# Gathers of four features for 32 batch rows each, released chunk by chunk, with the first half's layers 2 and 3 moved among the last chunks of a DLRM tower

## The reference

```
e = stack([tbl_f[ids[:, f]] for f in 0..25], axis=1)        # 512 x 26 x 128
combined = concatenate([dense[:, None, :], e], axis=1)       # 512 x 27 x 128
inter = einsum('bfd,bgd->bfg', combined, combined)
z = concatenate([dense, inter[:, iu, ju]], axis=1)           # pairs i < j
h = concatenate([z, dense], axis=1)                          # 512 x 607
h = maximum(h @ W_top1 + b_top1, 0)                          # 512
h = maximum(h @ W_top2 + b_top2, 0)                          # 256
y = h @ W_top3                                               # 1
```

## Time and profile before

| | |
|---|---|
| time, median of 3 runs | 138.34 us (137.31 to 138.55) |
| the profiled execution's span | 161.6 us |
| PE busy in it | 113.8 us (70%), 674 matmuls |
| PEld busy | 98.9 us (61%) |
| DVE busy | 85.1 us (53%) |
| POOL busy | 71.7 us (44%), 64 gathers among it |
| ACT busy | 65.7 us (41%) |
| mean granted TensorE clock | 0.873 of full speed |

### The profile page before, as it was taken

The page is one execution under the profiler, slowest core; times in us unless marked ns, Lnnn a source line. Parts: engine busy times, 40 slices in busy tenths (PEclk is TensorE's granted clock), DMA queues, the critical chain, the costliest instruction groups (busy, mean ns, idle before and its releaser), DMA issues.

```text
span 161.6 us, 1858 instructions
## 1 busy us (share of the span) xinstructions
PE 113.8 (70%) x674; PEld 98.9 (61%) x674; DVE 85.1 (53%) x162; ACT 65.7 (41%) x109; POOL 71.7 (44%) x72
## 2 busy tenths in 40 slices
PE   5499996995980997580000798762999697944994
PEld 5378774884860885570000897761999666943992
DVE  5399989997896370010000648966055731365031
ACT  3286994894894050200000657362133341332112
POOL 2687787878778777777770055710000000000000
PEclk9999999999998589967555569999699999996599
DMA  4998974797396221122110001110000000000000
GB/s 108 234 370 322 253 252 119 214 232 209 88 398 227 62 56 49 49 54 60 49 49 16 0 16 49 41 28 0 0 0 4 0 0 0 4 0 0 0 0 1
DMA packets 6331, 14.59 MB, mean 90 GB/s; under 512 B 1842, under 2 KB 2354, under 8 KB 6195
## 3 DMA queue, kind: packets, MB, share of 16 engines
q1 hardware_dynamic: 4130, 10.23, 20.4%
q0 software_dynamic: 2048, 4.20, 9.7%
q10 hardware_dynamic: 144, 0.05, 0.2%
HBM read 14.47 MB, written 0.00 MB: 90 GB/s over the span
## 4 chain that ended last, share of the span: by engine, by line
PE 34%; POOL 21%; issue 13%; another core or an unknown queue 11%; DVE 9%; DMA 6%; ACT 4%; DVEq 0%; ACTq 0%
POOL e_rows L345 21%; PE gram L413 15%; PE late L453 8%; DMA e_rows<-in_tbl,idx 3%; DMA idx<-in_ids_rows 2%; PE look L395 2%; DVE flip L748 2%; DVE flat L750 2%; ACT pT_hi L561 2%; PE late L385 2%; PE look L474 1%; PE late L386 1%; DVE dots L543 1%; ACT dots L561 1%
## 5 line engine op out<-in xcount | busy, mean ns | idle before, releaser
L345 POOL DMA_INDIRECT e_rows<-in_tbl,idx x64 | 70.8, 1107 | 33.0 <-issue 18.6
L413 PE MATMUL gram<-eT 128*123 128x108 f32 x256 | 32.9, 294 | 23.0 <-DVE dots L543 19.3
L413 PEld LDWEIGHTS gram<-eT 128*123 128x123 f32 x256 | 32.1, 210 | 23.8 <-ACT dots L561 17.9
L385 PE MATMUL late<-onehot,table_hi 128*128 128x512 f32 x84 | 35.3, 420 | 4.0 <-DVE table_lo L684 2.4
L691 DVE TENSOR_SCALAR onehot<-ids,row_of_partition 128x512 fp32r<-128x512 int32 x72 | 30.4, 483 | 7.5 <-PE late L386 5.8
L386 PE MATMUL late<-onehot,table_lo 128*128 128x512 f32 x84 | 34.1, 406 | 0.0
L543 DVE COPY dots<-gram 32x216 f32<-32x216 f32 (+1 forms) x32 | 12.3, 384 | 30.9 <-remote 18.3
L561 ACT ACTIVATE dots<-gram 32x216 f32<-32x216 f32 x32 | 10.9, 340 | 40.2 <-remote 22.2
L385 PEld LDWEIGHTS late<-onehot,table_hi 128*128 128x128 f32 x84 | 16.6, 198 | 8.4 <-ACT table_hi L561 2.7
L386 PEld LDWEIGHTS late<-onehot,table_lo 128*128 128x128 f32 x84 | 16.7, 198 | 3.2
L395 PE MATMUL look<-ident,e_rows 128*128 128x128 f32 x64 | 10.7, 294 | 6.7 <-DMA e_rows<-in_tbl,idx 6.3
(11 more groups left out here) (51 smaller groups left out, 110.2 us busy)
## 6 DMA issues: line engine op xcount, KB each, us to landing
table<-in_tbl SPq DMA_DIRECT2D x7, 512.0 KB
ids<-in_ids_bcast SPq DMA_DIRECT2D x10, 256.0 KB
table<-in_tbl SPq DMA_DIRECT2D x2, 640.0 KB
w_raw<-in_w SPq DMA_DIRECT2D x1, 1280.0 KB
e_rows<-in_tbl,idx POOLq DMA_INDIRECT x64
table<-in_tbl SPq DMA_DIRECT2D x2, 256.0 KB, 5.7
w_raw<-in_w SPq DMA_DIRECT2D x1, 512.0 KB
x_rows<-in_dense SPq DMA_DIRECT2D x1, 256.0 KB
```

The lines of the kernel that those rows point to most:

```text
L345: pool.indirect_dma_start(out=e_rows[:, n % GROUPS_AHEAD, s % GROUP, :], out_offset=None, in_=tables[f][:, :], in_offset=bass.IndirectOffs ...
L385: pe.matmul(bank, table_hi[0:KP, i % 2, c, :], hot, start=c == 0, stop=False)
L413: last = pe.matmul(gram[0:ROWS_OUT, n % 2, q, 0:QUADS * NG_COL], eT_flat[:, b * SLOTS:b * SLOTS + ROWS_OUT], eT[:, b:b + QUADS, 0:NG_COL], ...
```

## The change

Each gather now fetches, for 32 batch rows, four features: 128 rows again, from one table `gathered` in which the 16 tables stand one behind the other. Four gathers make a group, and group c holds all 16 features of chunk c. The host orders the ids that way and gives each feature's first row beside them; DVE adds the two before the first gather. `gram_chunk(n)` replaces `gram_tile(t)` and waits for the groups up to n alone. Groups 0 to 4 are turned behind tables 1 to 5, groups 5 to 7 behind tables 7 to 9, the others among the chunks. Layer 3 uses the `look` banks. The orders of PE, ACT and DVE behind the tables are written anew. DVE's and ACT's loops over tables use `AFTER_TABLE` in the same places where they used `EARLY`, and `w_split(k)` is the weight splitting that stood in `dots_tile`.

```diff
 
-GROUP, GROUPS_AHEAD = 4, 5
-GROUPS = [list(range(a, min(a + GROUP, NG))) for a in range(0, NG, GROUP)]
-NGR = len(GROUPS)
+GROUPS_AHEAD = 5
+UNIT = 32
+NCK = B // UNIT
+PER_GATHER = P // UNIT
+GROUP = NG // PER_GATHER
+assert GROUP * PER_GATHER == NG and NG * UNIT == B
...
-ALL_GROUPS = [(t, g) for t in range(TILES) for g in range(NGR)]
-FIRST_TABLE = 1
-EARLY = ALL_GROUPS[:NOH - FIRST_TABLE]
-REST = {t: [(t, g) for g in range(NGR) if (t, g) not in EARLY] for t in range(TILES)}
-
-AFTER_TABLES = [g for t in range(TILES) for g in REST[t]]
-assert len(AFTER_TABLES) == 7
-BESIDE_GRAM = {0: [None, None, AFTER_TABLES[0], None], 1: [None, AFTER_TABLES[1], None, None],
-               2: [AFTER_TABLES[3], None, None, AFTER_TABLES[4]], 3: []}
-AFTER_DENSE, AFTER_LAYER2, LAST_GROUPS = AFTER_TABLES[2:3], AFTER_TABLES[5:6], AFTER_TABLES[6:]
-
-
-def looks(ks):
-    return [("group", *k) for k in ks if k]
-
-
-LOOK_ORDER = [("dense",)] + looks(EARLY) + looks(BESIDE_GRAM[0]) + looks(BESIDE_GRAM[1])
-LOOK_ORDER += [("turn", 0)] + looks(AFTER_DENSE) + [("turn", 1)] + looks(BESIDE_GRAM[2])
-LOOK_ORDER += [("layer2", 0, n) for n in range(N2)] + looks(AFTER_LAYER2) + [("turn", 2)] + looks(LAST_GROUPS)
-LOOK_ORDER += [("turn", 3)] + [("layer2", 1, n) for n in range(N2)]
+AFTER_TABLE = {1: 0, 2: 1, 3: 2, 4: 3, 5: 4, 7: 5, 8: 6, 9: 7}
+
+
+LOOK_ORDER = [("dense",)] + [("group", c) for c in AFTER_TABLE.values()]
+LOOK_ORDER += [("group", 8), ("group", 9), ("turn", 0), ("group", 10), ("group", 11), ("turn", 1)]
+LOOK_ORDER += [("group", 12), ("turn", 2), ("layer2", 0, 0), ("layer2", 0, 1), ("group", 13), ("layer3", 0)]
+LOOK_ORDER += [("group", 14), ("group", 15), ("turn", 3)]
+LOOK_ORDER += [("layer2", 1, 0), ("layer2", 1, 1), ("layer3", 1)]
 LOOK = {what: n for n, what in enumerate(LOOK_ORDER)}
-assert FIRST_TABLE == 1 and all(("group", *k) in LOOK for k in ALL_GROUPS)
+assert [k[1] for k in LOOK_ORDER if k[0] == "group"] == list(range(NCK))
 
...
 for _h in range(HALVES):
-    LATE_ORDER += [("layer1", _h, 0), ("layer1", _h, 1), ("layer3", _h)]
+    LATE_ORDER += [("layer1", _h, 0), ("layer1", _h, 1)]
 LATE = {what: n for n, what in enumerate(LATE_ORDER)}
...
-            pool.wait_ge(idx_in, 16)
-            for t, g in ALL_GROUPS:
-                n = t * NGR + g
-                if n >= GROUPS_AHEAD:
-                    wait_look_full(pool, ("group", *ALL_GROUPS[n - GROUPS_AHEAD]))
-                for s in GROUPS[g]:
-                    f = GATHERED[s]
+            pool.wait_ge(idx_ready, 1)
+            for c in range(NCK):
+                if c >= GROUPS_AHEAD:
+                    wait_look_full(pool, ("group", c - GROUPS_AHEAD))
+                for k in range(GROUP):
+                    n = c * GROUP + k
                     pool.indirect_dma_start(
-                        out=e_rows[:, n % GROUPS_AHEAD, s % GROUP, :], out_offset=None, in_=tables[f][:, :],
-                        in_offset=bass.IndirectOffsetOnAxis(ap=idx[:, t, f:f + 1], axis=0)
-                    ).then_inc(rows_in[t][g], 16)
+                        out=e_rows[:, c % GROUPS_AHEAD, k, :], out_offset=None, in_=gathered[:, :],
+                        in_offset=bass.IndirectOffsetOnAxis(ap=idx[:, n:n + 1], axis=0)
+                    ).then_inc(rows_in[c], 16)
...
-            def turn_group(t, g):
-                bank = look_bank(("group", t, g))
-                pe.wait_ge(rows_in[t][g], 16 * len(GROUPS[g]))
-                for k, s in enumerate(GROUPS[g]):
-                    last = pe.transpose(bank[:, k * P:(k + 1) * P], e_rows[:, (t * NGR + g) % GROUPS_AHEAD, k, :], ident[:, :])
+            def turn_group(c):
+                bank = look_bank(("group", c))
+                pe.wait_ge(rows_in[c], 16 * GROUP)
+                for k in range(GROUP):
+                    last = pe.transpose(bank[:, k * P:(k + 1) * P], e_rows[:, c % GROUPS_AHEAD, k, :], ident[:, :])
                 last.then_inc(look_full, 1)
 
-            def gram_tile(t):
-
-                upto = LOOK["group", t, NGR - 1]
-                if t == 0:
+            def gram_chunk(n):
+
+                upto = LOOK["group", n]
+                if n == 0:
                     wait_late_done(pe, ("table", NOH - 1))
                     pe.wait_ge(pads_ready, 1)
                 pe.wait_ge(look_act, len([w for w in LOOK_ACT if LOOK[w] <= upto]))
                 pe.wait_ge(look_dve, len([w for w in LOOK_DVE if LOOK[w] <= upto]))
-                for c in range(NCH):
-                    n = t * NCH + c
-                    if n >= 2:
-                        pe.wait_ge(dots_act, n - 1)
-                        pe.wait_ge(dots_dve, n - 1)
-                    for q in range(CHUNK_Q):
-                        b = t * P + (c * CHUNK_Q + q) * QUADS
-                        last = pe.matmul(gram[0:ROWS_OUT, n % 2, q, 0:QUADS * NG_COL],
-                                         eT_flat[:, b * SLOTS:b * SLOTS + ROWS_OUT],
-                                         eT[:, b:b + QUADS, 0:NG_COL], start=True, stop=True)
-                    last.then_inc(gram_full, 1)
-                    if c < len(BESIDE_GRAM[t]) and BESIDE_GRAM[t][c]:
-                        turn_group(*BESIDE_GRAM[t][c])
+                if n >= 2:
+                    pe.wait_ge(dots_act, n - 1)
+                    pe.wait_ge(dots_dve, n - 1)
+                for q in range(CHUNK_Q):
+                    b = n * UNIT + q * QUADS
+                    last = pe.matmul(gram[0:ROWS_OUT, n % 2, q, 0:QUADS * NG_COL],
+                                     eT_flat[:, b * SLOTS:b * SLOTS + ROWS_OUT],
+                                     eT[:, b:b + QUADS, 0:NG_COL], start=True, stop=True)
+                last.then_inc(gram_full, 1)
...
-                bank = late_bank(("layer3", h))
+                bank = look_bank(("layer3", h))
...
+                if i == 0:
                     turn_dense()
-            gram_tile(0)
-            gram_tile(1)
+            gram_chunk(0)
+            gram_chunk(1)
+            turn_group(8)
+            gram_chunk(2)
+            gram_chunk(3)
+            gram_chunk(4)
+            gram_chunk(5)
+            turn_group(9)
+            gram_chunk(6)
             turn_pairs(0)
+            gram_chunk(7)
+            turn_group(10)
+            gram_chunk(8)
+            gram_chunk(9)
+            turn_group(11)
+            gram_chunk(10)
+            turn_pairs(1)
             layer1_dense(0)
-            groups(AFTER_DENSE)
-            turn_pairs(1)
+            gram_chunk(11)
             layer1_pairs(0)
-            gram_tile(2)
+            turn_group(12)
+            gram_chunk(12)
+            turn_pairs(2)
             layer2(0)
-            groups(AFTER_LAYER2)
-            turn_pairs(2)
+            turn_group(13)
+            gram_chunk(13)
             layer3(0)
             layer1_dense(1)
-            groups(LAST_GROUPS)
-            gram_tile(3)
+            turn_group(14)
+            gram_chunk(14)
+            turn_group(15)
+            gram_chunk(15)
             turn_pairs(3)
             layer1_pairs(1)
             layer2(1)
             layer3(1)
...
-            copy(eT[:, t * P:(t + 1) * P, s:s + n],
-                 look[:, LOOK[what] % 2, 0:n * P].rearrange("d (f b) -> d b f", f=n)).then_inc(done, 1)
+            copy(eT[:, c * UNIT:(c + 1) * UNIT, 1:1 + NG],
+                 look[:, LOOK[what] % 2, :].rearrange("d (f b) -> d b f", f=NG)).then_inc(done, 1)
...
                                    ACT.Relu, bias=b2_sb[:, n:n + 1]).then_inc(look_act, 1)
 
-            dots_tile(0)
-            dots_tile(1)
+            for n in range(6):
+                dots_chunk(n)
+                w_split(n)
+            group(9)
+            dots_chunk(6)
+            w_split(6)
             turn_hi(0)
-            groups(AFTER_DENSE)
+            dots_chunk(7)
+            w_split(7)
+            dots_chunk(8)
+            dots_chunk(9)
+            group(11)
+            dots_chunk(10)
             turn_hi(1)
+            dots_chunk(11)
             h1_split(0)
-            dots_tile(2)
+            dots_chunk(12)
+            turn_hi(2)
             h2_relu(0)
-            groups(AFTER_LAYER2)
-            turn_hi(2)
-            groups(LAST_GROUPS)
-            dots_tile(3)
+            group(13)
+            dots_chunk(13)
+            dots_chunk(14)
+            group(15)
+            dots_chunk(15)
             turn_hi(3)
             h1_split(1)
...
+            dve.wait_ge(idx_in, 16)
+            dve.tensor_tensor(idx[:, :], idx_parts[:, 0, :], idx_parts[:, 1, :], ALU.add).then_inc(idx_ready, 1)
...
-                wait_late_full(dve, ("layer3", h))
-                copy(y[0:1, h * HB:(h + 1) * HB], late[0:1, LATE["layer3", h] % 2, 0:HB]).then_inc(late_dve, 1)
-
-            dots_tile(0)
+                wait_look_full(dve, ("layer3", h))
+                copy(y[0:1, h * HB:(h + 1) * HB], look[0:1, LOOK["layer3", h] % 2, 0:HB]).then_inc(look_dve, 1)
+
```

(43 more changed lines are left out.)

103 lines of the change are left out of this document (47 added, 56 removed).

## The result

The changed kernel takes 135.62 us in the median (132.2 to 138.84, 4 runs) beside 138.44 for the kernel before (137.31 to 138.66, 4 runs): a ratio of 0.966, 95% interval 0.954 to 0.977. It is faster, by 2.8 us in the median where 4.9 were forecast, and its runs lie much further apart than those of the kernel before. The profiled execution was the shortest, 132.2 us, with a span of 130.2 us.

What follows compares the result with a forecast made beforehand. PE was taken as bound by gathers up to Gram, then by waits for DVE and ACT. -5.9 for Gram's start and +1.0 for waits make -4.9: 138.34 becomes 133.4, forecast's own range 131.9 to 134.9, whole range 130.2 to 139.0.

Steps and rivals of the forecast that it cites:

- The start of Gram: End of the tables: one group less turned there moves Gram from 64.3 to 58.4, -5.9, between -7.0 and -3.7.
- The last link: Before Gram: group 7's rows land at 57.9, are turned by 58.3, and Gram starts at 58.4.
- The add: DVE's index addition of 64 integers per partition before the gathers: delays all of them by 0.2 us.
- The 4.15: At table 8: transposes of 0.4 and 16 products at 0.23 at full clock, against 6.7 us in the trace.
- The waits: PE behind Gram's start: 9.6 us removed, 10.2 added, 0.4 for one more group; net +1.0, from -1.5 to +3.
- group 8: Turned behind chunk 1: rows land at 63.1, PE is there at 62.0, a wait of 1.1 us.
- rival A: PE's clock falls again behind new waits, 1.7 to 2.3 per spell: 135.4 with one, 137.5 with two; chance 0.2.
- a stretch of 0.7: Gathers 30 and 31 beside table 9's one-hots on DVE take 0.35 longer each, 0.7 together, range 0 to 1.4.
- put together: The kernel before, its profile reckoned without the stop: Gram at 64.3, span 137.1 instead of 161.6.
- C: Rival: the 4.33 us wait before table 8 isn't in the timed runs, so 139.0; chance 0.13.
- D: Rival: gathers from one table of some 187,000 rows lose pace; 0.3 more per gather gives 143; chance 0.10.
- B: Rival: new waits overlap better (-1.5) or gathers land in 2 us (-1): 131; chance 0.15.

Runs made afterwards that it cites:

- before, again: The kernel before, unchanged, run and profiled a second time: 139.0 us, span 137.3.
- shift alone: The kernel before with only group 5 turned behind table 7, 6 behind 8, 7 behind 9, 8 behind chunk 1: 136.64 us median beside 139.13.
- nine groups: The changed kernel with nine groups turned behind tables 1 to 9 as before, all else kept: 140.34 us median, ratio 1.020.
- changed, second: The changed kernel, unchanged, run and profiled again: 135.47 us median (7 runs) beside 139.13, ratio 0.974; profiled span 137.2.
- old order: The changed kernel with the order behind the tables put nearly back to that of the kernel before: 135.38 us, ratio 0.984.
- new order: The changed kernel with layer 2(0) moved ahead of group 12 and the turning of pairs 2: 132.0 us, ratio 0.960.
- group 4 later: The changed kernel with group 4 turned behind table 6 instead of table 5: 137.88 us, ratio 0.978.
- best: The changed kernel with layer 2(0) earlier, group 13's copy ahead of turn_hi(2) on ACT, and identity products in PE's waits: 131.52 us beside 138.01.

## Why the prediction was right, and where its sizes were off

| kernel | 32nd gather's issue ends | Gram starts | Gram to the end | span |
|---|---|---|---|---|
| before, again | 55.00 | 64.89 | 72.4 | 137.3 |
| shift alone | 54.20 | 56.62 | 78.7 | 135.3 |
| nine groups | 52.21 | 61.88 | 74.4 | 136.3 |
| changed, first | 53.57 | 56.55 | 73.65 | 130.2 |
| changed, second | 57.30 | 60.75 | 76.45 | 137.2 |
| old order | 54.79 | 57.22 | 74.3 | 131.5 |
| new order | 54.13 | 57.21 | 72.3 | 129.5 |
| group 4 later | 58.30 | 60.95 | 76.9 | 137.8 |
| best | 54.61 | 57.20 | 69.7 | 126.9 |

**The start of Gram.** -5.9 forecast, -8.3 in the first profile (64.89 to 56.55), -4.1 in the second: the second inside the bounds of 3.7 and 7.0, the first beyond them. The main mechanism is as told: the long wait and the half clock behind it are gone in the first profile. The last link isn't. The forecast let Gram's start hang on the rows of group 7, the 32nd gather. Gram does begin 2.4 to 3.5 us behind that gather's issue in all rows of the table with eight groups, but PE waits for group 7 for 0.37 us at most (the shift alone), and in neither profile of the changed kernel. There the last wait for rows is that for group 6 (0.78, first) or for group 4 (4.39, second); behind it come PE's own tables and ACT's copy of table 9. In the first profile all of this was early: the turning of group 6 began at 51.13 (52.5 reckoned), and table 9's copy ended at 56.50 (57.9). The issue of the 32nd gather ended 1.7 us earlier than reckoned (53.57 for 55.24), although one of the gathers beside the last one-hots took 2.02; the turning then began 1.7 us behind it where I had taken 2.7.

**The add** took 0.23 us (0.2 forecast), and the first gather starts at 4.85 (5.1). The 4.15 that the prediction has for group 6's turning and table 8 at full clock is 4.1 by its own terms (0.4 and 16 x 0.23); nothing hangs on the difference.

**The waits.** 10.02 us for the forecast's 10.2; Gram to the end 73.65 for 73.8. That is partly luck in the parts: chunks 6 and 10 and layer 2 wait longer (1.48, 1.88, 2.49 for 0.8, 1.3, 2.0), group 8 and chunk 13 less (0 and 0.72 for 1.1 each); chunks 12, 14 and 15 are within 0.2 (1.62, 0.83, 1.00 for 1.8, 0.85, 1.2). Group 8 was in time: its rows were there by 60.27, where I had 63.1, and 1.7 us of that is how early the gathers were. That the order costs about what it saves fits the kernels with one half of the change: nine groups with the new gathers, release and order are +1.2 in the median (+1.0 forecast), but the same three are -1.2 when they are added to the shift, and the order isn't to be seen when the old one is put back behind the new gathers. All three are near what six runs can tell.

**The clock, rival A.** The chance was too low, and the price of 1.7 to 2.3 for a spell a little too high. The forecast held against A that none of the new waits reaches 3.4 us alone. In the second profile the clock fell twice behind shorter ones, at chunk 10 and at layer 2(0), the second being a place that A names; such spells cost 1.4 to 1.6 us each in the profiles that have one. At layer 2(0), with the order as in the changed kernel, the wait of 2.45 to 2.49 was followed by one in three profiles of six. The same wait of 1.88 or 1.89 us before chunk 10 (1.90 in one) was followed by a chunk of 1.94 us in five profiles and of 2.22, 2.42, 2.94 and 3.51 us in four others; the wait of 3.48 before pairs 3 is followed by half clock in all twelve profiles in which PE is idle in it (the 36 products take 5.86 to 7.32 us) and in neither of the two in which it is kept busy (4.54 and 4.56). Whether a short wait is punished changes from execution to execution.

**What the forecast lacked.** It treated the gathers' pace as one number with a stretch of 0.7. A gather that is held up for 4.4 us was not in the trace of the kernel before, where the longest of those among the tables takes 2.41, and my range of 0 to 1.4 for the stretching was too small (the two gathers beside the last one-hots took 1.68 and 3.60 in the second profile, 3.4 more than twice 0.94). The second profile of the kernel before has such a gather too (4.39), and there it cost little: the 20th gather's issue ends at 36.87 instead of 35.93, the 32nd's at 55.00 instead of 54.34, and the span is the one put together without it. In the changed kernel's two profiles the 20th ends at 33.78 and at 37.34, the 32nd at 53.57 and at 57.30. But the 3.7 us at the 32nd are not what moves Gram: 2.7 of them are a second held gather, the 32nd itself (3.60 us), and it costs nothing, since PE still doesn't wait for group 7. The chain runs through group 4. Its last gather is the 20th; its turning begins at 41.17 instead of 37.48, 3.7 later, and the half clock behind that wait, less the 0.78 that PE no longer waits for group 6, adds the other 0.5. The timed median holds executions of both sorts, so what failed is the step from the sum for one execution to the median, where I took a constant difference. The shorter executions bear the sum out: the ratio of 0.966 is 4.7 us of 138.44, for the 4.9 forecast. The median of all, 135.62, lies outside the forecast's own 131.9 to 134.9 and beside A's 135.4; that the sum of the first profile's parts came out so near is no proof of its single terms.

**Rivals.** C fell by the second profile of the kernel before. D's reason fell: the gathers of one large table take as long as the old ones. Groups by line, first the shift alone with the old gathers, then the changed kernel:

```profile
L346 POOL DMA_INDIRECT e_rows<-in_tbl,idx x64 | 70.3, 1099 | 22.4 <-issue 18.9
```

```profile
L337 POOL DMA_INDIRECT e_rows<-in_gathered,idx x64 | 70.7, 1104 | 22.4 <-issue 18.6
```

B held in part in the first profile (the gathers landed earlier, by about the 1 us it names), not its better overlap. A and the held gather are what separates the second profile from the first. That they also make the 2.2 us between the median and the forecast is likely and not shown, nor how much of it is whose, since only two executions of the changed kernel have a trace. The stop in the first profile of the kernel before didn't come again in any of the 13 other traces, and its cause is open.

## What to carry to other kernels

Where a chain of transfers feeds the engine that sets the end, ask for each piece no sooner than the issuing engine can have it landed, and look at what comes behind: the shift alone started Gram 8.3 us earlier and shortened the span by 2.0. Of a wait on PE count the clock it costs; where there is a free bank and an operand that is there anyway, cheap products in the wait avoid it. And where a kernel's runs lie far apart, profile it twice before putting a sum on the median.
